# A transformer block, three batches in flight: the second norm's rows and one subtraction on GpSimd, and all four queues dealt anew

## The reference

```python
h = layernorm(x) * (1 + ca) + sa
x = x + ga * attention(h)          # rms norm, 16 heads of 64, causal softmax, gated, Wout
h = layernorm(x) * (1 + cb) + sb
x = x + gb * ffn(h)
```

## Time and profile before

| what | value |
|---|---|
| median of three runs | 1484.22 us (1483.99 to 1484.85) |
| the profiled execution | 1485.03 us, span 1483.2 us |
| mean granted TensorE clock | 0.991 of full speed |
| busy: TensorE, VectorE | 1415.4 us (95%), 1356.4 us (91%) |
| busy: ScalarE, GpSimd | 1247.8 us (84%), 1037.8 us (70%) |

### The profile page before, as it was taken

The page is one execution under the profiler, slowest core; times in us unless marked ns, Lnnn a source line. Parts: engine busy times, 40 slices in busy tenths (PEclk is TensorE's granted clock), DMA queues, the critical chain, the costliest instruction groups (busy, mean ns, idle before and its releaser), DMA issues.

```text
span 1483.2 us, 39666 instructions
## 1 busy us (share of the span) xinstructions
PE 1415.4 (95%) x11491; PEld 1162.9 (78%) x11491; DVE 1356.4 (91%) x5403; ACT 1247.8 (84%) x4114; POOL 1037.8 (70%) x1161
## 2 busy tenths in 40 slices
PE   5799999999999999999999999999999999999987
PEld 3677788788788778788888788888778878878877
DVE  4679999999999999999999999999999999999986
ACT  4788888988888888888898888898888888888872
POOL 0237787777787777787777778777778777778751
PEclk8999999999999999999999999999999999999998
DMA  4000000000000000000000000000000000000000
GB/s 122 22 14 16 10 20 19 19 16 16 7 19 19 19 16 19 9 14 19 19 16 19 14 9 19 19 17 19 14 9 19 19 19 16 18 5 23 13 10 10
DMA packets 50737, 27.74 MB, mean 19 GB/s; under 512 B 10288, under 2 KB 49904, under 8 KB 50704
## 3 DMA queue, kind: packets, MB, share of 16 engines
q1 hardware_dynamic: 50464, 26.91, 7.0%
q10 hardware_dynamic: 240, 0.43, 0.1%
HBM read 23.02 MB, written 4.31 MB: 18 GB/s over the span
## 4 chain that ended last, share of the span: by engine, by line
PE 63%; DVE 25%; issue 6%; ACT 5%; DMA 1%; POOL 0%; DVEq 0%; SPq 0%; POOLq 0%
PE pS L1309 9%; PE pW L1245 9%; PE pW L1247 7%; PE pW L1246 7%; PE pW L1322 6%; PE pS L1299 5%; DVE h L1017 5%; DVE pS L935 4%; PE pS L1295 4%; ACT pS L616 4%; PE pW L1393 4%; PE pW L1390 4%; PE pW L1326 2%; DVE p_sb L955 2%; PE pW L1381 2%
## 5 line engine op out<-in xcount | busy, mean ns | idle before, releaser
L616 ACT ACTIVATE pS<-pS,nmx 128x128 f32<-128x128 f32 (+1 forms) x1024 | 390.5, 441 | 53.6 <-DVE nmx L935 53.6
L484 POOL TENSOR_TENSOR fexp<-fexp,fsum 128x512 f32<-128x512 f32 x240 | 300.3, 1284 | 76.8 <-DVE fexp L1055 76.8
L935 DVE CUSTOM_DVE_ANT_0 pS<-pS,mask 128x128 f32<-128x128 f32 (+1 forms) x1024 | 330.2, 390 | 22.4 <-PE pS L1299 21.5
L475 POOL TENSOR_TENSOR fsum<-ex 128x512 f32<-128x512 f32 x252 | 255.1, 1050 | 0.0
L608 ACT COPY pT<-pS 128x768 f32<-128x768 f32 x256 | 211.7, 827 | 35.6 <-PE pS L1309 31.3
L1309 PE MATMUL pS<-ident,p_sb 128*128 128x128 f32 x1536 | 215.9, 277 | 9.7 <-DVE p_sb L955 6.7
L955 DVE TENSOR_TENSOR p_sb<-pS,coef 128x256 f32<-128x256 f32 (+2 forms) x512 | 210.5, 453 | 8.9
L1309 PEld LDWEIGHTS pS<-ident,p_sb 128*128 128x128 f32 x1536 | 173.0, 141 | 40.2 <-issue 12.8
L616 ACT ACTIVATION_READ_ACCUMULATOR pS<-pS,nmx 128x1 f32 x1024 | 202.5, 198 | 0.0
L598 ACT COPY qk<-pW 128x512 f32<-128x512 f32 x256 | 166.5, 651 | 7.9 <-PE pW L1247 7.8
L1322 PE MATMUL pW<-pT,v 128*64 128x256 f32 x1024 | 165.3, 401 | 0.7 <-ACT pT L608 0.6
(11 more groups left out here) (186 smaller groups left out, 3673.9 us busy)
## 6 DMA issues: line engine op xcount, KB each, us to landing
x_in<-in_L_attn_tokens SPq DMA_DIRECT2D x32, 128.0 KB, 2.2
x_res<-in_L_attn_tokens SPq DMA_DIRECT2D x32, 128.0 KB, 3.0
modB<-mods_dram SPq DMA_DIRECT2D x32, 128.0 KB, 2.9
out<-yo SPq DMA_DIRECT2D x32, 128.0 KB, 1.9
modA<-mods_dram SPq DMA_DIRECT2D x31, 128.0 KB, 3.1
modC<-mods_dram SPq DMA_DIRECT2D x32, 64.0 KB, 3.2
fsum<-in_L_attn_Wkv SPq DMA_DIRECT2D x2, 512.0 KB, 8.9
fsum<-in_L_attn_Wq SPq DMA_DIRECT2D x1, 512.0 KB, 7.8
```

The source lines that it names most:

```text
L475: ins = nc.gpsimd.tensor_tensor(fsum[:, k, h], ex[:, k, h, 0:NX].unsqueeze(2).broadcast_to([P, NX, NK]), ex[:, k, RH + h, :].unsqueeze(1). ...
L484: ins = nc.gpsimd.tensor_tensor(fexp[:, k, h, :], fexp[:, k, h, :], fsum[:, k, h].rearrange("p i j -> p (i j)"), ALU.mult)
L616: ins = nc.scalar.activation(ps, ps, ACT.Exp, bias=nmx[:, p % 2, h, k:k + 1], scale=-1.0, accum_out=den(p)[:, h, k:k + 1])
L935: ins = nc.vector.tensor_tensor_reduce(out=ps, in0=ps, in1=mask[:, (1 - k) * P:2 * P], scale=-1.0, scalar=LARGEST, op0=ALU.add, op1=ALU.mi ...
```

## The change

GpSimd's `rstd2` becomes `normalise2`, which goes on to write `h2` itself, and `ln2_modulate` is gone from VectorE. The shift of the eight largest, `top_d`, is a GpSimd step `shift_tops`, for which VectorE counts `top_s_ready`. The list `order`, and with it the banks, is dealt anew, and so are the orders of ScalarE, VectorE and TensorE. Two short chains of semaphores change their lengths.

```diff
-        order = [("V", 0, 0), ("QK", 2, 0), ("QK", 3, 0), ("V", 3, 0), ("PV", 6, -1), ("GU", 1, -2),
-                 ("PV", 7, -1), ("D", 0, -2), ("V", 1, 0), ("D", 1, -2), ("GU", 2, -2), ("op", 0, -1),
-                 ("PV", 0, 0), ("PV", 1, 0), ("QK", 4, 0), ("GU", 3, -2), ("QK", 5, 0), ("V", 4, 0),
-                 ("hT", 0, -1), ("PV", 2, 0), ("QK", 6, 0), ("V", 2, 0), ("sim", 0, -1), ("V", 5, 0),
-                 ("QK", 7, 0), ("PV", 3, 0), ("sim", 1, -1), ("ET", 0, -2), ("PV", 4, 0), ("PV", 5, 0),
-                 ("xT", 0, 1), ("ET", 1, -2), ("y", 0, -2), ("GU", 0, -1), ("QK", 0, 1), ("QK", 1, 1)]
+        order = [("V", 0, 0), ("PV", 6, -1), ("QK", 2, 0), ("V", 3, 0), ("QK", 3, 0), ("GU", 1, -2),
+                 ("V", 1, 0), ("PV", 7, -1), ("D", 0, -2), ("V", 4, 0), ("D", 1, -2), ("GU", 2, -2),
+                 ("op", 0, -1), ("PV", 0, 0), ("PV", 1, 0), ("QK", 4, 0), ("GU", 3, -2), ("QK", 5, 0),
+                 ("V", 2, 0), ("hT", 0, -1), ("PV", 2, 0), ("PV", 3, 0), ("QK", 6, 0), ("sim", 0, -1),
+                 ("V", 5, 0), ("QK", 7, 0), ("ET", 0, -2), ("sim", 1, -1), ("PV", 4, 0), ("PV", 5, 0),
+                 ("xT", 0, 1), ("y", 0, -2), ("ET", 1, -2), ("GU", 0, -1), ("QK", 0, 1), ("QK", 1, 1)]
...
+                def shift_tops():
+                    if w.live(-1):
+                        pool.wait_ge(S(top_s_ready), at(top_s_ready, f, TB))
+                        t = top_s[:, :, :, :].rearrange("p a h n -> p (a h) n")
+                        nc.gpsimd.tensor_tensor(top_d[:, :, :, :].rearrange("p a h n -> p (a h) n"), t, t[:, :, 0:1].broadcast_to([P, 2 * TB * RH, TK]),
+                                                ALU.subtract).then_inc(S(top_d_ready), 1)
...
-                def rstd2():
+                def normalise2():
...
-                        nc.gpsimd.tensor_tensor(rs2[:, :], ve2[:, :], expo[:, :], ALU.pow).then_inc(S(rstd2_out), 1)
+                        nc.gpsimd.tensor_tensor(rs2[:, :], ve2[:, :], expo[:, :], ALU.pow).then_inc(S(pool_chain2), 1)
+                        pool.wait_ge(S(pool_chain2), at(pool_chain2, f, 2))
+                        apart()
+                        for k in range(TB):
+                            ins = nc.gpsimd.tensor_scalar(h2[:, k, :], x2[:, k, :], mv2[:, k, 0:1], rs2[:, k:k + 1], ALU.subtract, ALU.mult)
+                        ins.then_inc(S(h2_ready), 1)
...
                 fold(0)
-                rstd2()
+                normalise2()
                 weigh(1)
                 rstd1()
                 add_heads(1)
                 rms1()
+                shift_tops()
                 fold(1)
...
-                def ln2_modulate():
-                    if w.live(-1):
-                        dve.wait_ge(S(rstd2_out), at(rstd2_out, f, 1))
-                        for k in range(TB):
-                            ins = nc.vector.tensor_scalar(h2[:, k, :], x2[:, k, :], mv2[:, k, 0:1], rs2[:, k:k + 1], ALU.subtract, ALU.mult)
-                        ins.then_inc(S(h2_ready), 1)
...
-                        link(ins, head_chain, f)
+                        ins.then_inc(S(top_s_ready), 1)
+                        dve.wait_ge(S(top_s_ready), at(top_s_ready, f, k + 1))
...
-                        if k == TB - 1:
-                            nc.vector.tensor_tensor(top_d[:, :, :, :], top_s[:, :, :, :], top_s[:, :, :, 0:1].broadcast_to([P, 2, TB * RH, TK]),
-                                                    ALU.subtract).then_inc(S(top_d_ready), 1)
-                            done(head_chain)
```

ScalarE's order, from the first pair's scale to pair 3's outputs:

```diff
                 exp_scores(3)
-                copy_transposes(2, 0)
                 weighted(1)
+                gate_up(3)
                 queries(4)
                 scale_head(3)
-                gate_up(3)
+                copy_transposes(2, 0)
                 queries(5)
+                values(2)
                 copy_transposes(3, 0)
-                values(4)
                 modulate_h()
                 high_part(h2T_high, h2T, "hT")
                 exp_scores(4)
+                weighted(2)
+                exp_scores(5)
+                weighted(3)
+                scale_head(5)
                 queries(6)
-                weighted(2)
-                values(2)
-                exp_scores(5)
+                values(5)
                 queries(7)
-                values(5)
-                scale_head(5)
-                weighted(3)
```

VectorE's order:

```diff
                 normalise(1)
+                choose(1, 0)
                 gated_down(0)
-                choose(1, 0)
+                choose(1, 1)
+                row_max(2)
+                bias_product(2)
+                row_max(3)
+                ln2_stats()
                 gated_down(1)
-                row_max(2)
-                row_max(3)
-                bias_product(2)
+                gate_product(2)
                 normalise(2)
-                ln2_stats()
-                gate_product(2)
-                choose(1, 1)
                 normalise(3)
                 ln1_stats()
-                ln2_modulate()
...
                 normalise(4)
+                normalise(5)
                 shift(0)
-                normalise(5)
                 ln1_modulate()
...
                 finish()
+                normalise(7)
                 bias_product(0)
-                normalise(7)
                 gate_product(0)
```

TensorE's order:

```diff
                 transpose_scores(7, -1)
+                weigh_values(6)
                 project_qk(2)
-                project_qk(3)
                 project_v(3)
                 scores(1)
-                weigh_values(6)
+                project_qk(3)
                 gate_up(1)
+                project_v(1)
                 weigh_values(7)
                 project_down(0)
-                project_v(1)
                 transpose_scores(0, 0)
+                project_v(4)
                 project_down(1)
                 gate_up(2)
...
                 weigh_values(1)
-                transpose_scores(2, 0)
                 project_qk(4)
                 gate_up(3)
                 project_qk(5)
-                project_v(4)
+                project_v(2)
+                transpose_scores(2, 0)
+                transpose_h()
                 transpose_scores(3, 0)
                 scores(4)
-                transpose_h()
                 scores(5)
                 weigh_values(2)
+                weigh_values(3)
                 project_qk(6)
-                project_v(2)
                 similarity(0)
                 project_v(5)
                 project_qk(7)
-                weigh_values(3)
                 transpose_scores(4, 0)
-                similarity(1)
                 transpose_scores(5, 0)
                 transpose_experts(0)
+                similarity(1)
...
+                project_ffn(0)
                 transpose_experts(1)
-                project_ffn(0)
                 project_ffn(1)
```

More of the change, by code:

```diff
@@ L203, in program @@
         rstd1_in, rstd1_out = ev("rstd1_in", 2), ev("rstd1_out", 2)
-        pool_chain1, pool_chain2 = ev("pool_chain1", 2), ev("pool_chain2", 1)
+        pool_chain1, pool_chain2 = ev("pool_chain1", 2), ev("pool_chain2", 2)
         xr_ready = ev("xr_ready", 1)
@@ L211, in program @@
         x2g_ready = ev("x2g_ready", 1)
-        rstd2_in, rstd2_out = ev("rstd2_in", 1), ev("rstd2_out", 1)
+        rstd2_in = ev("rstd2_in", 1)
         h2_ready = ev("h2_ready", 1)
-        top_d_ready, tops_ready = ev("top_d_ready", 1), ev("tops_ready", 1)
+        top_s_ready, top_d_ready, tops_ready = ev("top_s_ready", TB), ev("top_d_ready", 1), ev("tops_ready", 1)
         cand_ready, rz_ready = ev("cand_ready", 1), ev("rz_ready", 1)
@@ L740, in body @@
                 copy_transposes(7, -1)
+                values(0)
+                weighted(6)
                 queries(2)
-                values(0)
+                values(3)
+                exp_scores(0)
                 queries(3)
-                exp_scores(0)
-                weighted(6)
-                values(3)
                 gate_up(1)
@@ L749, in body @@
                 weighted(7)
+                values(1)
+                scale_head(1)
                 down_tanh(0)
-                scale_head(1)
                 copy_transposes(0, 0)
+                copy_transposes(1, 0)
                 down_tanh(1)
-                copy_transposes(1, 0)
+                values(4)
                 gate_up(2)
-                values(1)
                 exp_scores(2)
@@ L782, in body @@
                 total(1)
+                experts(0)
                 weighted(4)
@@ L785, in body @@
                 rms_scale()
-                experts(0)
                 expert_exp(1)
@@ L789, in body @@
                 weighted(5)
+                exp_scores(6)
                 experts(1)
-                exp_scores(6)
                 exp_scores(7)
@@ L1011, in ln2_stats @@
                         ins.then_inc(S(rstd2_in), 1)
-                def ln2_modulate():
-                    if w.live(-1):
```

(7 more changed lines are left out.)

## The result

The changed kernel takes 1533.13 us (1532.68 to 1533.82, four runs) where the one before took 1484.11 beside it (1482.60 to 1484.85, four runs): ratio 1.0333, 95% interval 1.032 to 1.0346. The forecast of 1501 had the direction right and the size a third of what came; 1533 lies above its range. The profiled execution took 1533.45, its span 1531.5, which is 48.3 above the span before.

The account below looks back on a forecast made before the run. TensorE was taken as the bound, with 1.5 to 2 us of a pass lost to VectorE. Stretches of 0.53 + 1.19 - 1.16 = +0.56 a pass, +16.8 over 30 passes on 1484.2, gave 1501 us; range 1478 to 1518.

Parts of the forecast that it names:

- stretch 1: TensorE's queue from pass start to project_out: +0.53 for V4 now in it, other small terms cancelling.
- stretch 3: TensorE's queue from similarity 0 to the pass's end: -1.16, as PV3 leaves (-0.76) and small savings come.
- The two waits: TensorE stands still 1.81 us at PV1 for gated_down(1), and 0.88 at S5 for ScalarE's copy 3.
- stretch 2: TensorE's queue from project_out to similarity 0: from 14.81 to 16.00 us, +1.19.
- the 0.1 less of waiting at S3: In stretch 1, a little less waiting at S3 (about -0.1) cancels one more change between kinds of products (about +0.1).
- the 0.2 for restarts and changes of kind saved: In stretch 3, restarts behind waits and changes of kind saved: -0.2, an estimate between 0 and -0.4.
- the two transpositions that no longer meet: In stretch 3, ET1 no longer follows transpose_x: -0.2.
- Nothing new is late: In stretch 3, QK7's copy comes about 0.4 ahead of its turn, shift(0) for the second similarity about 0.2 ahead.
- The moved arithmetic: VectorE loses 3.65 us a pass; GpSimd's three instructions take 0.45 each, hidden with over 2 us to spare.
- The choosing instructions: Rival, the lock: GpSimd's adds make VectorE 0.67 late at ln2_stats, PV1 waits 2.5; +1.2 a pass, 1521; chance 0.11.
- The relief of VectorE: Rival: all TensorE's waits on VectorE go, 1.5 us a pass, 1439; chance 0.03.
- The faster case: Rival: ScalarE keeps up, S5 waits only 0.2; -0.2 a pass, 1478; chance 0.18.

Follow-up runs that it names:

- e1: The changed kernel with gated_down(1) and gate_product(2) ahead of ln2_stats on VectorE: 1490.70 us, ratio 1.0046.
- e2: The changed kernel with ScalarE's gate_up(3) behind scale_head(3), copies of pairs 2 and 3 together, values(2) behind them: 1533.52 us, ratio 1.0332.
- e3: The changed kernel with choose(1, 1) back behind gate_product(2) on VectorE: 1532.92 us, ratio 1.0319.
- e8: e2 with PV3's outputs copied ahead of exponent 5 on ScalarE (weighted(3) ahead of exp_scores(5)): 1545.62 us, ratio 1.0413.
- e9: e8 with VectorE's shift(0) ahead of normalise(5) and TensorE's similarity(1) between transpose_scores(4) and transpose_scores(5): 1575.14 us, ratio 1.0606.
- e7: The changed kernel with the norm's rows back on VectorE, behind ln1_stats: 1543.53 us, ratio 1.0405.
- e5: e1 with e8's ScalarE order and transpose_h behind S4 on TensorE: 1510.69 us, ratio 1.018.
- e11: e5 with shift(0) ahead of normalise(5) and similarity(1) between transpose_scores(4) and transpose_scores(5): 1532.00 us, ratio 1.031.
- e12: e1 with gate_product(2) put back behind ln2_stats, gated_down(1) still ahead of it: 1507.61 us, ratio 1.0142.
- the three in the old order: e4, e6, and e6 with gate_product(2) ahead of normalise(2) on VectorE: 1490.19, 1463.49 and 1469.64 us.
- e4: The kernel before, in its old orders, with only the norm's rows and the shift of the eight largest moved to GpSimd: 1490.19 us, ratio 1.003.
- e6: e4 with transpose_experts(1) behind project_ffn(0), its bank dealt after y's, ScalarE's experts(1) behind exp_scores(6): 1463.49 us, ratio 0.9863.

## Why the prediction was wrong

In microseconds from the start of `project_out`, or as the length of a stretch:

```
point                        predicted  measured
PV1 starts                       6.27      6.37
S4 starts                       11.41     11.72
S5 starts                       12.94     13.29
similarity 0 starts             16.00     16.41
stretch 1 (13.32 before)        13.85     14.02
stretch 3 (15.99 before)        14.83     15.01
pass                            44.67     45.45
```

(A stretch 1 of 13.32 is 724.00, the start of V0, to 737.32 in the kernel before, and 15.99 is 752.13 to the next V0 at 768.12. The measured steps are the differences of the starts shown above.)

**The two waits were right in place and size.** PV1's gap was to be 1.81 and is 718.23 - 715.63 - 0.70 = 1.9; S5's was to be 0.88 and is 725.15 - 723.58 - 0.65 = 0.92. Place, releaser and reason are those of the text, and e1 shows that undoing the first takes away most of the loss. That the second, as a cost, fits was luck: without it (e2) the pass is as long, since QK7 then waits instead.

**The step that failed first is the sum of stretch lengths around them**, which was made to 0.1 us from terms that were not known to 0.1. Stretch 1 is 0.17 over, PV1 to S4 0.21 over, PV1's own start 0.10, the rest of stretch 2 another 0.10, and stretch 3 gives back 0.98 instead of 1.16. All err on one side: a pass was to gain 0.56 and gained 1.34, so 0.78 x 30 = 23 us.

The terms behind this can be read from the starts. In stretch 1 V4 takes 707.82 - 707.21 = 0.61 where the sum had 0.53, and the 0.1 less of waiting at S3 did not come: S2 to S3 is 1.05 in both kernels. In stretch 2 the sum let the statistics begin with `project_out`'s delivery, and they begin 0.14 behind it (0.13 in e3, where VectorE stands waiting); `transpose_h` and T3 take 0.31 and 0.83 where it had 0.24 and 0.75. In stretch 3 the 0.2 for restarts and changes of kind saved came to some 0.03, while the two transpositions that no longer meet gave 0.3 instead of 0.2.

The one wait among them is a mechanism that the forecast had wrong: "Nothing new is late" in stretch 3. QK7 was held to have its copy 0.4 ahead of its turn. By the forecast's own numbers its turn comes at 16.00 + 1.39 = 17.39 (1.39 from similarity 0 to QK7 as in the kernel before), 5.98 behind S4, so the chain from S4 over exponents 4 and 5 to that copy was taken as 5.6 us; it is 6.17, QK7 comes 0.16 late (V5 to QK7 is 0.78 us, where it was 0.62), and its weights wait, in the waits of the changed kernel (600 to 1000 us):

```profile
PEld pW L1247 <- ACT aoT L612: 3.3, 8, 0.4
```

The forecast took each wait as a delay of TensorE alone, but a late S4 makes the exponents late, and with them PV3's copy, `normalise(5)` and `shift(0)`; e2, e8 and e9 show that chain from its several ends.

**The second step was not in the text at all: the clock.** Six low stretches cost 9 us. They stand in all kernels with the gap at PV1 but e7 (the changed one, e2, e3, e8, e9) and in none without it (e1, e5, e11, e12, and the three in the old order). So the gap goes with them here but is not enough by itself. 23 + 9 = 32 is the distance from 1501 to 1533.

**The moved arithmetic** took 0.40 for `top_d` (0.45 estimated), but 0.80 for each row of `h2`, over the bound of 0.75. GpSimd was to be done with the norm 2.1 us behind the statistics (1.5 to 2.7); it is done 721.10 - 717.60 = 3.5 behind, in part because it begins 0.68 late, behind `fold(0)`, which the forecast did not count. So 1.3 us were to spare ahead of `transpose_h`, not over 2. In the changed kernel it was hidden, as said; e1 shows where that cover ends, 0.62 at `transpose_h` once the rows come 0.3 later and TensorE 1.8 sooner. That `shift_tops` delays `fold(1)` at no cost because `transpose_experts(1)` moves is what e4 against e6 confirms in the old order: 27 us hang on that move.

**The rivals.** The choosing instructions are slow beside GpSimd's adds (2.24 and 2.30 for two), but that cost nothing: `row_max(3)` ends at 715.86, 0.16 behind the delivery, but e3, with VectorE 1.58 early, begins the statistics no sooner. The relief of VectorE was refused at 0.03 because "PV1's wait follows from the order", rightly for this diff; e6 shows that it was there to be had, 0.72 of the 1.5 us a pass. The faster case named S5's wait as what decides; e2 refutes that, as S5's wait can go without a gain.

**What stays open.** e1 has the changed orders without PV1's wait and runs 44.36 a pass, e6 has the old ones and runs 43.39. Where that microsecond stands can be read from the stretches (medians; e1, then e6): V0 to `project_out` 14.03 and 13.31, on to similarity 0 14.79 and 13.97, on to the next V0 15.54 and 16.12. With V4 (0.6) having moved into the first stretch out of the second and PV3 (0.8) into the second out of the third, e1 loses about 0.1, 0.6 and 0.2. The 0.6 is the size of the wait at `transpose_h`, and the third holds QK7's. But e5, which moved the work around both waits, only made others, so whether these orders can be had without that loss is not settled.

## What to carry to other kernels

A piece of work that gives a buffer back has a deadline of its own: before putting a piece that waits (here the statistics, for `project_out`) ahead of it, look up who takes that buffer next and when, once for each piece behind the wait. Move arithmetic to an idle engine first and alone, and then follow what stands behind it in that engine's queue: here one transposition moved behind sixteen products turned 5 us of loss into 20 of gain, and the rest of the reordering cost 70. A queue that is full on three engines answers an edit with the next wait in the ring, so a sum of tenths of a microsecond needs a margin on the side of loss, and an edit that removes a wait is not yet a gain.

## What the runs showed of the hardware

TensorE's clock fell to 1.2 GHz for 3.4 us at a time in the middle of a run, in six of 30 passes, about 1 us behind a gap of 1.9 us in an otherwise filled queue; each fall cost 1.55 us. With no gap at PV1 (e1, e5, e11) or with one of 1.1 us behind it instead (e12) the granted clock was 1.00 from 100 to 1440 us, and in e7, with the gap as long, too; what decides it was not found.

What the choices of the earlier trace rows meet reaches small rows too: a VectorE instruction of 128x128 with two scalars per partition takes 0.33 us with GpSimd idle and up to 1.43 beside GpSimd's 128x512 adds. The Trainium skill, page "SBUF — State Buffer", section "SBUF: two separate sides", says that a GpSimd instruction and a VectorE instruction that uses two ports or two SBUF inputs hold a shared pair of ports as an exclusive lock, whichever starts first. These rows agree, 1.43 against 0.33. The same rows of `h2` took GpSimd 0.80 each, and VectorE 1.08 to 1.30 in the kernel before, where the adds of GpSimd ran beside them.
